# A gated attention block with routed experts: contexts and shifted scores side by side, other PSUM banks, one division per batch

## The reference

```python
x = x + tanh(g_xattn) * attention(layernorm(x), ctx)       # 16 heads of 8 features, softmax over 128 keys
x = x + tanh(g_ffn) * experts(layernorm(x))                # 8 experts, hidden 512
# attention: q = ln(x) @ Wq + bq; k, v = ctx @ Wk + bk, ctx @ Wv + bv; softmax(q k^T * 8**-0.5) v, then @ W_out + b_out
# experts: softmax over 8 logits, each token goes to its largest one, at most 512 tokens per expert in token order;
#          relu(x @ W1 + b1) @ W2 + b2, times the gate
```

## Time and profile before

| | |
|---|---|
| median of 3 runs | 298.25 us (296.54 to 298.52) |
| profiled execution | 298.6 us, of which the span of the profile is 296.5 |
| mean granted clock of TensorE | 0.937 of full speed |
| busy: PE, DVE, POOL, ACT | 244.5, 196.6, 182.3, 155.6 us |
| maxima (L833) | 81.6 us in 128 instructions |
| exponentials (L703) | 72.0 us in 128 instructions |

### The profile page before, as it was taken

The page is one execution under the profiler, slowest core; times in us unless marked ns, Lnnn a source line. Parts: engine busy times, 40 slices in busy tenths (PEclk is TensorE's granted clock), DMA queues, the critical chain, the costliest instruction groups (busy, mean ns, idle before and its releaser), DMA issues.

```text
span 296.5 us, 8184 instructions
## 1 busy us (share of the span) xinstructions
PE 244.5 (82%) x2907; PEld 163.5 (55%) x2907; DVE 196.6 (66%) x663; ACT 155.6 (52%) x375; POOL 182.3 (61%) x246
## 2 busy tenths in 40 slices
PE   1748758788979989999899989995869999999950
PEld 1325525465755755765656666663324677777740
DVE  4676717647978999989897999965302545555440
ACT  5553727567778787787887756681202322222100
POOL 6625916911982998897897968448720056555781
PEclk9998959969999999999999999999595999999995
DMA  4652771990482652661733541138352256554310
GB/s 120 184 162 73 214 217 32 237 293 19 113 235 57 174 158 71 195 182 46 213 110 90 152 126 57 58 102 174 138 144 66 71 170 188 173 180 132 103 55 16
DMA packets 50920, 39.27 MB, mean 132 GB/s; under 512 B 9698, under 2 KB 47223, under 8 KB 50880
## 3 DMA queue, kind: packets, MB, share of 16 engines
q1 hardware_dynamic: 47168, 28.67, 35.9%
q0 software_dynamic: 3712, 10.07, 10.4%
HBM read 13.72 MB, written 12.65 MB: 89 GB/s over the span
## 4 chain that ended last, share of the span: by engine, by line
PE 39%; DVE 13%; DMA 13%; SPq 10%; issue 9%; ACT 8%; POOL 4%; POOLq 0%; ACTq 0%; DVEq 0%
PE X L634 9%; DMA qp<-mrow 8%; DVE negm L833 6%; SPq L347 6%; PE TS L618 5%; PE M L546 3%; ACT prob L703 3%; PE O L513 3%; PE TS L497 3%; PE O L618 3%; PE M L618 2%; PE S L482 2%; PE X L441 2%; SPq L358 2%; POOL rec_dram L1224 2%
## 5 line engine op out<-in xcount | busy, mean ns | idle before, releaser
L703 ACT ACTIVATE prob<-TS 128x512 f32<-128x512 f32 x128 | 72.0, 589 | 40.1 <-PE TS L497 39.2
L833 DVE TENSOR_REDUCE negm<-S 128x4 f32<-128x512 f32 x128 | 81.6, 679 | 8.5 <-PE S L482 7.9
L513 PE MATMUL O<-prob,vals 128*32 128x128 f32 x1024 | 42.1, 283 | 0.8 <-ACT oraw L712 0.8
L1313 POOL DMA_INDIRECT out_dram<-fin,tok x32 | 31.5, 986 | 14.2 <-issue 12.2
L1224 POOL DMA_INDIRECT rec_dram<-rec,slot x32 | 32.2, 1005 | 8.0 <-issue 5.5
L497 PE MATMUL TS<-qp,kp 64*128 64x128 bf16 x512 | 28.1, 221 | 9.7 <-DMA qp<-mrow 9.6
L482 PE MATMUL S<-kp,qp 62*128 62x128 bf16 x512 | 31.3, 222 | 2.3 <-DVE negm L833 2.0
L513 PEld LDWEIGHTS O<-prob,vals 128*32 128x32 f32 x1024 | 24.6, 110 | 13.9 <-ACT prob L703 7.0
L267 POOL TENSOR_TENSOR rest_k<-full_k,parts_k 128x512 f32<-128x512 f32 x7 | 8.0, 1149 | 39.3 <-ACT parts_k L674 39.3
L804 ACT ACTIVATE qp<-TS,b_act 128x512 f32<-128x512 f32 x16 | 11.0, 687 | 39.9 <-PE TS L618 39.9
L634 PE MATMUL X<-w2s,qp 128*128 128x128 f32 x240 | 28.2, 275 | 0.9 <-issue 0.9
(11 more groups left out here) (170 smaller groups left out, 486.8 us busy)
## 6 DMA issues: line engine op xcount, KB each, us to landing
kp<-parts_k SPq DMA_DIRECT2D x48, 128.0 KB, 2.5
qp<-parts_q SPq DMA_DIRECT2D x48, 128.0 KB, 4.1
rec_dram<-zeros POOLq DMA_DIRECT2D x8, 516.0 KB, 6.2
xr<-rec_dram SPq DMA_DIRECT2D x8, 260.0 KB, 3.9
x_sb<-in_x_dram SPq DMA_DIRECT2D x8, 256.0 KB, 3.6
c_sb<-in_ctx_dram SPq DMA_DIRECT2D x8, 256.0 KB, 3.5
out_dram<-rec SPq DMA_DIRECT2D x8, 256.0 KB, 3.3
w1s<-in_L_ffn_W_dram SPq DMA_DIRECT2D x8, 256.0 KB, 4.1
```

Source lines behind the costliest of these rows:

```text
L513: mm = nc.tensor.matmul(o_out[i * HV:(i + 1) * HV, u * L:(u + 1) * L], vals[G % 2][:, k, h, :], prob[n % 2][:, h * L:(h + 1) * L], start=( ...
L703: nc.scalar.activation(prob[n % 2][:, first:first + 4 * L], TS[:, a, :], ACT.Exp).then_inc(a_exp, 1)
L833: V.tensor_reduce(negm[n % 2][:, first:first + 4], S[:, a, :].rearrange("p (h k) -> p h k", k=L), AX.X, ALU.max, negate=True).then_inc(v_r ...
L1313: G_.indirect_dma_start(out_rows, bass.IndirectOffsetOnAxis(tok[p][:, t:t + 1], 0), fin[p][:, t, :], None, bounds_check=T - 1, oob_is_err= ...
```

## The change

TensorE's order in a step becomes: scores 0, shifted 0, values 0, `m`, `oT` of the batch five steps back, group tasks, scores 1, shifted 1, values 1, `back`, `at`, group tasks. So `oT` moves to step n + 5, ahead of `at` in the second half, and takes its bank: `X[:, 0]` has `oT` and `at`, `M` has `m` and `back`, and the tasks `xT` and `q` go to `X[:, 1]` (in the first two groups, ahead of the loop, they stay in `X[:, 0]`). ScalarE copies `oraw` at the end of step n + 3 in place of the start of n + 4, and `onT` in the first half of n + 5. VectorE runs normalise and residual behind the second maxima. The columns of Wq, Wk, their biases and the values are dealt out so that the two sets of heads alternate; with that, normalise has one product of 128 columns in place of two of 64. SyncE's store moves from `j == 0` to `j == 1`, and GpSimd's scatters wait for `v_m` in place of `v_x1`.

```diff
-            bank0 = [("at", c - 5), second]
-            bank1 = [first, third]
-            bank2 = [("m", c - 1), ("back", c - 4), ("oT", c - 4)]
+            bank0 = [second] if c < 0 else [("oT", c - 5), ("at", c - 5)]
+            bank1 = [first, third] if c < 0 else [first, third, second]
+            bank2 = [("m", c - 1), ("back", c - 4)]
...
-        oT_out = M[:, 0, 2 * L:3 * L]
+        oT_out = X[:, 0, 0:L]
+        AHEAD = 2
...
+
+        def q_bank(H):
+
+            return X[:, 0 if H < AHEAD else 1, :]
...
-                loads, stores = j == 0 and is_group(g + 2), j == 0 and is_group(g - 2)
+                loads, stores = j == 0 and is_group(g + 2), j == 1 and is_group(g - 2)
...
-                        mm = nc.tensor.transpose(X[:, 0, k * L:(k + 1) * L], xn[:, k, :], ident)
+                        mm = nc.tensor.transpose(q_bank(idx)[:, k * L:(k + 1) * L], xn[:, k, :], ident)
...
-                    nc.tensor.matmul(X[:, 0, :], wq_dh[:], xnT[idx % 2][:], start=True, stop=True).then_inc(p_q, 1)
+                    nc.tensor.matmul(q_bank(idx), wq_dh[:], xnT[idx % 2][:], start=True, stop=True).then_inc(p_q, 1)
...
                 if is_batch(c - 2):
                     shifted(c - 2, 0)
+                if is_batch(c - 3):
+                    values(c - 3, 0, 0)
+                    values(c - 3, 0, 1)
                 if is_batch(c - 1):
                     bank_free(pe, "m", c - 1)
                     pe.wait_ge(v_red, 4 * c)
                     nc.tensor.transpose(m_out, negm[(c - 1) % 2][:], ident).then_inc(p_m, 1)
+                if is_batch(c - 5):
+                    bank_free(pe, "oT", c - 5)
+                    pe.wait_ge(v_on, c - 4)
+                    nc.tensor.transpose(oT_out, on[(c - 5) % 2][:], ident).then_inc(p_oT, 1)
                 for t in at_q[0]:
                     group_task(t[0], t[1])
-                if is_batch(c - 5):
-                    bank_free(pe, "at", c - 5)
-                    pe.wait_ge(a_oT, c - 4)
-                    nc.tensor.matmul(X[:, 0, 0:DE], onT[(c - 5) % 2][:], wout_g[:], start=True, stop=True).then_inc(p_at, 1)
+                if is_batch(c):
+                    scores(c, 1)
+                if is_batch(c - 2):
+                    shifted(c - 2, 1)
                 if is_batch(c - 3):
-                    values(c - 3, 0, 0)
-                    values(c - 3, 0, 1)
+                    values(c - 3, 1, 0)
+                    values(c - 3, 1, 1)
                 if is_batch(c - 4):
                     bank_free(pe, "back", c - 4)
...
                         mm = nc.tensor.transpose(back_out[:, u * L:(u + 1) * L], oraw[(c - 4) % 2][:, u * L:(u + 1) * L], ident)
                     mm.then_inc(p_back, 1)
-                if is_batch(c):
-                    scores(c, 1)
-                if is_batch(c - 2):
-                    shifted(c - 2, 1)
+                if is_batch(c - 5):
+                    bank_free(pe, "at", c - 5)
+                    pe.wait_ge(a_oT, c - 4)
+                    nc.tensor.matmul(X[:, 0, 0:DE], onT[(c - 5) % 2][:], wout_g[:], start=True, stop=True).then_inc(p_at, 1)
                 for t in at_q[2]:
                     group_task(t[0], t[1])
-                if is_batch(c - 3):
-                    values(c - 3, 1, 0)
-                    values(c - 3, 1, 1)
                 for t in at_q[3]:
                     group_task(t[0], t[1])
-                if is_batch(c - 4):
-                    bank_free(pe, "oT", c - 4)
-                    pe.wait_ge(v_on, c - 3)
-                    nc.tensor.transpose(oT_out, on[(c - 4) % 2][:], ident).then_inc(p_oT, 1)
                 if c == -6:
                     pe.wait_ge(s_wg, 16)
...
-                nc.scalar.activation(full[side][:], X[:, side, :], ACT.Identity, bias=bias,
+                nc.scalar.activation(full[side][:], X[:, 1, :] if side else q_bank(H), ACT.Identity, bias=bias,
...
-                    val = X[:, 1, :].rearrange("p (k h d) -> p k h d", k=GB, d=HD)[:, :, a * HH:(a + 1) * HH, :]
+                    val = X[:, 1, :].rearrange("p (k h a d) -> p k h a d", k=GB, a=2, d=HD)[:, :, :, a, :]
...
                 j, g = c % GB, c // GB
-                if is_batch(c - 4):
-                    n = c - 4
-                    act.wait_ge(p_O, n + 1)
-                    if n >= 2:
-                        act.wait_ge(p_back, n - 1)
-                    nc.scalar.activation(oraw[n % 2][:], o_out, ACT.Copy).then_inc(a_O, 1)
                 if is_batch(c - 2):
...
                     exps(c - 2, 0, 1)
+                if is_batch(c - 5):
+                    n = c - 5
+                    act.wait_ge(p_oT, n + 1)
+                    if n >= 2:
+                        act.wait_ge(p_at, n - 1)
+                    nc.scalar.activation(onT[n % 2][:], oT_out, ACT.Copy).then_inc(a_oT, 1)
                 if j == (2 if g + 2 else 1) and is_group(g + 2):
...
                     exps(c - 2, 1, 1)
+                if is_batch(c - 3):
+                    n = c - 3
+                    act.wait_ge(p_O, n + 1)
+                    if n >= 2:
+                        act.wait_ge(p_back, n - 1)
+                    nc.scalar.activation(oraw[n % 2][:], o_out, ACT.Copy).then_inc(a_O, 1)
                 if j == 2 and is_group(g + 2):
...
                         act.wait_ge(p_xl, H - 1)
-                    nc.scalar.activation(xnT[H % 2][:], X[:, 0, :], ACT.Copy).then_inc(a_xT, 1)
+                    nc.scalar.activation(xnT[H % 2][:], q_bank(H), ACT.Copy).then_inc(a_xT, 1)
                 if j == 3 and is_group(g + 2):
...
                     first_part(0, g + 2)
-                if is_batch(c - 4):
-                    n = c - 4
-                    act.wait_ge(p_oT, n + 1)
-                    if n >= 2:
-                        act.wait_ge(p_at, n - 1)
-                    nc.scalar.activation(onT[n % 2][:], oT_out, ACT.Copy).then_inc(a_oT, 1)
                 if j == 1 and g + 2 == 0:
...
-            def normalise(n, G):
-                o = back_out.rearrange("p (h a v) -> p a h v", a=2, v=HV // 2)
+            def normalise(n):
+                o = back_out.rearrange("p (h v) -> p h v", v=HV // 2)
...
-                V.reciprocal(rl[:].rearrange("p (a h) -> p a h", a=2), o[:, :, :, HD]).then_inc(v_rl, 1)
+                V.reciprocal(rl[:], o[:, :, HD]).then_inc(v_rl, 1)
...
-                if G is not None:
-                    moments2_ready(G)
-                for a in range(2):
-                    mm = V.tensor_tensor(on[n % 2][:, a * HALF:(a + 1) * HALF].rearrange("p (h d) -> p h d", d=HD),
-                                         o[:, a, :, 0:HD],
-                                         rl[:, a * HH:(a + 1) * HH].unsqueeze(2).broadcast_to([P, HH, HD]), ALU.mult)
-                mm.then_inc(v_on, 1)
+                V.tensor_tensor(on[n % 2][:].rearrange("p (h d) -> p h d", d=HD), o[:, :, 0:HD],
+                                rl[:].unsqueeze(2).broadcast_to([P, HEADS, HD]), ALU.mult).then_inc(v_on, 1)
...
-                              wqkv[:, D:2 * D].rearrange("p (a h d) -> p a d h", a=2, d=HD))
+                              wqkv[:, D:2 * D].rearrange("p (h a d) -> p a d h", a=2, d=HD))
...
-                              wqkv[:, 0:D].rearrange("p (a h d) -> p a d h", a=2, d=HD)).then_inc(s_vset, 1)
+                              wqkv[:, 0:D].rearrange("p (h a d) -> p a d h", a=2, d=HD)).then_inc(s_vset, 1)
...
                     lower_part(c - 1)
-                if is_batch(c - 5):
-                    residual(c - 5)
-                if is_batch(c - 4):
-                    normalise(c - 4, g - 2 if j == 0 and is_group(g - 2) else None)
-                if j == 0 and is_group(g - 2) and g - 2 < NG - 1:
-                    moments2(g - 2)
-                if c == B + 4:
-                    route2(NG - 1)
-                    place2(NG - 1)
                 if c == -7:
...
+                if is_batch(c - 4):
+                    normalise(c - 4)
+                if is_batch(c - 5):
+                    residual(c - 5)
+                if j == 0 and is_group(g - 2) and g - 2 < NG - 1:
+                    moments2_ready(g - 2)
+                    moments2(g - 2)
+                if c == B + 4:
+                    route2(NG - 1)
+                    place2(NG - 1)
...
-                    pool.wait_ge(v_x1, min(c - 4, B))
+                    pool.wait_ge(v_m, min(c, B))
...
```

More of the change, by code:

```diff
@@ L300, in _ @@
                 for a in range(2):
-                    at = i * D + a * HALF
                     sp.dma_start(bqk[a * HALF:(a + 1) * HALF, i:i + 1],
-                                 b_qkv[at:at + HALF].rearrange("(h d o) -> d h o", d=HD, o=1),
+                                 b_qkv[i * D:(i + 1) * D].rearrange("(h a d o) -> a d h o", a=2, d=HD, o=1)[a],
                                  allow_slow_non_contiguous=True).then_inc(s_bias, 16)
```

## The result

The changed kernel takes 307.03 us (median of 4 runs, 304.67 to 310.76), the kernel before 298.38. The ratio is 1.0292, 95% interval 1.0227 to 1.0357: slower by 2.9%, 8.6 us, outside the range that was forecast and on the other side. The profiled execution of the changed kernel lasted 310.8 us, 3.7 more than the median; it and those of experiments 3, 5 and 7 were among the slow ones of their kernels, which the ratios leave out. Its rows show the losses larger than the runs do, so they stand beside the profile of experiment 4: that kernel differs from the changed one in the place of one transposition alone, takes the same time (ratio 1.0288), and its profiled execution lasted 306.2 us. Sizes rest on ratios of runs, places on the rows.

The account below looks back on a forecast made before the run. The prediction took VectorE's own queue of work to bound the kernel, with TensorE and the maxima's DMA close behind. Its terms, -2.0 - 5.0 + 3.7 + 2.1 - 1.3, gave -2.5 us, so 296.1 us, range 290 to 303.

Parts of the forecast that it names:

- They meet: Second half of a step: `back` ready and VectorE's maxima done, both 1.6 us after the scores begin.
- term 2: VectorE's waits for `back` (3.7) and projection (2.3) go, less 1.0 of new holes: -5.0 us.
- I take 2.8 off and 1.5 back: Waits for the maxima's DMA and the context shrink by 2.8 us; later maxima behind the moved store cost 1.5.
- term 5: Store one step later on SyncE's queue, freeing the second step's maxima and the context load: -1.3 us.
- Term 1: VectorE's normalise: one product of 128 columns per batch in place of two of 64: -2.0 us.
- 0 if every step gets a hole of 0.2: Unfavourable end for the removal of VectorE's waits for `back` and projection: small holes in every step leave no gain.
- Term 3: The maxima's path: transposition behind contexts on TensorE delays ScalarE's copy and the shifted scores: +3.7 us.
- Term 4: First half short for VectorE, long for TensorE: holes before the second maxima, 0.3 per group: +2.1 us.
- second rival: Second half's scores come too late, so VectorE waits between lower part and second maxima: 303.1 us, chance 0.20.
- third rival: On SyncE's queue the store stands in front of the third step's maxima: 304.3 us, chance 0.05.
- the moments' place: norm2's moments come about 1.5 us later, costed at nothing; 1.5 us per group if POOL (GpSimd) were idle.

Follow-up runs that it names:

- experiment 3: Changed kernel with the second half's scores ahead of the group tasks on TensorE: 316.63 us.
- experiment 5: Changed kernel with its store at j == 3 and `back` ahead of the second half's products with the values: 306.58 us, ratio to before 1.0184.
- experiment 7: Kernel before with its store moved from j == 0 to j == 3: 297.17 us, ratio to before 0.9927.
- experiment 4: Changed kernel with the maxima's transposition `m` back ahead of the first half's contexts: 306.69 us, ratio to before 1.0288.
- experiment 1: Changed kernel with its store moved from j == 1 to j == 3: 303.22 us, ratio to before 1.0143.
- experiment 2: Kernel before with its store alone moved from j == 0 to j == 1: 300.3 us, ratio to before 1.0125.
- experiment 8: Changed kernel, store at j == 1 but of 8 of 128 partitions, 16 KB in place of 256: 303.57 us, ratio to before 1.0077.
- experiment 9: Changed kernel, store at j == 3, `back` and output projection both ahead of the second half's products with the values: 302.22 us, ratio to before 1.0095.
- experiment 11: Kernel before in its own order, with one product per batch, and store and both loads at j == 3: 291.65 us, ratio 0.9805.
- experiment 6: Kernel before with only one product of 128 columns per batch in place of two of 64: 297.71 us, ratio 0.9964.

## Why the prediction was wrong

Two steps failed: "They meet" in term 2 and "I take 2.8 off and 1.5 back" in term 5.

**Term 1 (-2.0)** holds in the rows: 0.35 became 0.29 us and the unwaited step shrank by 0.07. By runs it is 0.36% with an interval that reaches no change.

**Term 2 (-5.0) failed.** Its step was "They meet": `back` ready 1.6 us after the second scores begin, VectorE done at the same time. I counted both from the start of the scores. But the four matmuls of the second bank cannot start until the first maxima have left it, and all that follows on TensorE counts from there, while VectorE's clock runs from the first bank. In experiment 1's rows `back` is ready 2.2 us after the scores' start (99.00) and VectorE is done after 1.9. The wait for the projection went; the one for `back` grew to 7.1 us in 20 places (up to the last lower part 5.2 in experiment 4 and 7.3 in experiment 1), about the 6.0 that both had been. Counted in waits the term was -1 to +1 instead of -5, near its own other end, "0 if every step gets a hole of 0.2".

**Term 3 (+3.7)**: the wait for the copy grew from 7.5 to 9.8 us, 8.2 in experiment 4, and with the transposition back in its place (that is experiment 4) the time did not move. No run shows a cost of this size for it, and a smaller one could not be seen.

**Term 4 (+2.1)**: the wait for scores grew by 6.6 us (6.9 in experiment 4), with the store at j == 3 by 2.4. The size was about right while the shifted scores are on time. The second rival's place is the one that showed (over 8 us), and late maxima are what it said could take the lead away; what made them late is the third rival's store.

**Term 5 (-1.3) failed in its sign**: +1.25% in experiment 2, about 3.7 us, and 1.5% in the changed kernel. The step at fault is "I take 2.8 off and 1.5 back". Off came the step into j = 2, 4.52 to 4.18 in experiment 2; back came more, 5.45 to 5.98 into j = 0 and 5.63 to 5.90 into j = 3. The third step's maxima wait for the end of an unbroken queue, and one more row of 0.6 us stands in it. And the waiting can cost more than itself: in experiment 2 the shifted scores near 90 us waited 1.80 us where it had been 0.62, and the key projection behind them ran 1.91 us at a granted clock of 0.50 where it had taken 1.02. The third rival named the place and the direction, at 304.3 for 0.05 of the chance. Its reason, 1.8 us for 256 KB more in front of the maxima, is not what the rows show (2.64 us to the landing with them, 2.77 without, experiment 8). The Trainium skill's rule on the semaphore increment ("DMA: Bandwidth & Descriptors", Queues, rings and completion order) stood beside it. No run here shows it at work on the store; as a 256 KB load stands in front in each of the three cases, none contradicts it.

**Costed at nothing, wrongly:** the moments' place. The prediction named the condition, an idle GpSimd; it is met at the end of the attention, 1.6 us by the rows.

Summed by runs: 2.9% are 8.7 us; 3.7 of them come with the store's line alone (experiment 2), so 5.0 are left for everything else, the product's small gain included. In these 1.6 are the tail, and 0.4 in each of seven steps with the routing are the hole before the reciprocal. How the rest divides between `back`, scores and the copy isn't settled: experiments 3, 5 and 9 each removed one wait and another took its place.

## What to carry to other kernels

When two engines pass a double-banked buffer back and forth, time a schedule from the moment at which the last bank comes free, not from the first write. Count what stands on the queue ahead of a small transfer that a whole pipeline waits for; ask of each bulk transfer which step can wait longest, and put it there: here that was worth more than any order of the engines that was tried. Where two results for one engine come from one in-order queue, removing one wait moved it to the other each time here, so look at both before moving either.

## What the runs showed of the hardware

TensorE ran a key projection (two 512-column matmuls) at the lower of the clock's two levels, 1.2 GHz, behind idle stretches of 1.80 us (experiment 2, granted clock 0.50, 1.91 us), 2.07 (experiment 4, 0.50, 1.91 us) and 1.21 (experiment 11, 0.50, 1.91 us). Behind 1.77 us (experiment 4), 1.98 and 1.99 (experiment 8) and 2.55 (experiment 6) the same projection took 1.02. In experiment 2 TensorE had been busy at a granted clock of 1.00 up to the stretch. So the length of an idle stretch alone does not tell whether the clock falls behind it.

The maxima's small DMA landed 2.77 us after its issue's end behind a 256 KB load, 2.70 with a 16 KB store in front of that load, 2.64 and 2.86 with one of 256 KB, and 1.57 in the empty queue. A 256 KB store held SyncE's queue for 0.60 us, one of 16 KB for 0.49.
